# Biased maxima in two halves of the heads, the output gate beside them, and the last mixture chunks beside the first keys' products

## The chip, the core and the metric

One core of one Trainium2 chip runs the kernel. The metric is the device time in microseconds (us) of one execution. The engines have one queue each and run side by side: TensorE (PE), VectorE (DVE), ScalarE (ACT), GpSimd (POOL), and SyncE (SP), which issues the transfers. They wait for each other by semaphores only.

## The reference

Eight sequences of 512 tokens and 256 channels go through block attention, a layer norm, a mixture of experts, and a second layer norm.

```python
x = _layernorm(x + _L0_attn_ref(x, ...), axis=-1)
x = _layernorm(x + _L0_ffn_ref(x, ...), axis=-1)
# attention: 32 heads of 8 channels, chunks of 32 tokens
gate = jnp.einsum('bshd,bnhd->bhsn', q, kmean)     # own chunk always, future never
_, topk_idx = jax.lax.top_k(gate, 4)               # four chunks for each query and head
scores = jnp.where(allowed, jnp.einsum('bshd,bthd->bhst', q, k) * scale, NEG)
o = jnp.einsum('bhst,bthd->bshd', jax.nn.softmax(scores), v)
g = (hidden_states @ Wg1.T @ Wg2.T)
o = o * rms * o_norm_weight * jax.nn.sigmoid(g);  o = o @ Wo.T
# mixture: 2 shared and 16 routed experts of width 176, every expert on every token
hj = jax.nn.relu(flat @ w1 + b1); acc + (hj @ w2 + b2) * gating
```

## The kernel before

The program runs eight turns, one for each sequence. Turn b does the attention of sequence b and, woven into the same queues, the mixture of sequence m = b - 1. The first turn has no mixture (m is None), and after the eighth turn the last mixture runs alone. So seven turns have both. The order is written out by hand on each engine, and semaphores tie the queues together.

The mixture's hidden layer is cut into 25 chunks of 128 units. One chunk goes: `up`, in three parts of two products each, into one of two PSUM banks (`BK_H`, by the chunk's parity); `relu` on ScalarE; `gated` on VectorE, the multiplication with the expert's gate, whose rows come by transfer; `high` on ScalarE, the fp16 upper part; `low` on GpSimd, the rest; `down`, in four parts of three products, into the two output banks 6 and 7 (`BK_Y`).

The attention part of a turn has these stages.

- Selection of chunks (`best`, `select`), beside chunks 3 to 10.
- **Maxima**, beside chunks 11 to 21 (`C_MAX`). 40 units `max_unit` (eight groups of four heads, five units each) write query-by-key products into two pairs of banks in turn (`RING` is 2). VectorE reduces each unit to one maximum for every 32 keys (line 1356). `DEALT` lists the mixture's pieces, and `dealt(u)` is what follows unit u. `selection_rows` turns the selection's rows for the transfer.
- **The passage.** VectorE adds the selection's bias to the chunk maxima and takes the maximum, for four tiles j of 128 queries and 32 heads at once (lines 1365 and 1368). TensorE turns the four results (line 691) into PSUM, `maxima` on ScalarE copies them to `negT`, and SP moves them into the row `R_MAX` of `qET`, where the queries stand. The selection's rows go to `qET` too, once all maxima products are done (`bias_rows`). Beside it: the second factor of the output gate (line 682), its tanh (`output_gate`, line 956) and chunks 22 to 24 (`late_up`, `late_down`).
- **Keys.** 40 units `key_unit` write key-by-query products, with bias and maximum in them as extra rows. ScalarE takes the exponential (line 992, signal `act_p`), GpSimd clears what is above the diagonal (`causal`, line 1111, signal `pool_p`), and TensorE multiplies with the values (`outputs`, line 718). Two groups later `to_tokens` (line 728) turns a group's result, after VectorE has copied it (`copy_outputs`, line 1374, signal `dve_o`). `PAIRS` says which of three bank pairs a key unit uses, the third being the mixture's output banks 6 and 7; `BACK` says how many units earlier an exponential must be done. The third pair is used from group 1 on, after VectorE has read the mixture's result (`dve_z`).
- `finish` on VectorE: two reads of the mixture's result (line 1231), the layer norm's sums and inverse root, then `copy_outputs(0)`, then the scaling.

On GpSimd all `low` of a turn stand ahead of the first `stage` (line 1103, the values of a group) and `causal`.

## Time and profile before

| | us |
|---|---|
| median of 3 runs | 1453.25 (1452.52 to 1456.14) |
| the profiled execution, its own time | 1453.75 |
| its span, first to last instruction | 1451.7 |
| TensorE busy | 1332.4 (92%) |
| VectorE busy | 1087.7 (75%) |
| ScalarE busy | 842.7 (58%) |
| GpSimd busy | 533.9 (37%) |
| mean granted TensorE clock | 0.961 |

The time lies 2.05 us above the span. Busy shares are means over unlike stages; an engine of 75% can be the bound of one stage. A timeline row of several instructions gives the time from the first start to the last end. Ends of products are modelled and overlap the next start by about 0.06 us, so the cost of a piece is read from the start of one row to the start of the next. The first turn starts its keys at 122.4 us; the seven turns with a mixture follow each other at about 169 us. The last mixture alone ends at the span's end.

### The profile page before, as it was taken

How to read it: one execution, taken by the hardware profiler on the slowest of the kernel's cores; microseconds unless marked ns; L12 is line 12 of the kernel's file. 1: busy time of each engine (PE TensorE's matmuls, PEld its weight loads, DVE VectorE, ACT ScalarE, POOL GpSimd, SP SyncE). 2: the span in 40 equal slices, each digit the busy share in tenths (PEclk: the TensorE clock that was granted, in tenths of full speed). 3: DMA queues.
4: the chain of work that ended last, by engine and by line, in shares of the span. 5: the costliest groups of instructions: out<-in, count | busy, mean ns of one | idle time of the engine just before them, and what ended most of it. 6: DMA issues, size and time to landing. Idle time of an engine off the chain costs nothing.

```text
span 1451.7 us, 29057 instructions
## 1 busy us (share of the span) xinstructions
PE 1332.4 (92%) x10992; PEld 738.7 (51%) x10992; DVE 1087.7 (75%) x2747; ACT 842.7 (58%) x1266; POOL 533.9 (37%) x638
## 2 busy tenths in 40 slices
PE   5677999999998999999999999989999899999597
PEld 3422475535754366534755356543665347553364
DVE  6994688957897578966889578975889668885434
ACT  5406774396735876277743967358762877439121
POOL 3203542254323642245422553235432454225143
PEclk8667999999999999999999999999999999999799
DMA  6001022200321021210222003210112102220031
GB/s 243 16 15 17 16 79 76 52 17 16 104 66 38 30 59 60 74 31 16 82 71 55 16 17 102 71 33 30 60 62 71 31 16 68 73 53 23 13 113 58
DMA packets 52283, 77.81 MB, mean 54 GB/s; under 512 B 6334, under 2 KB 26800, under 8 KB 51888
## 3 DMA queue, kind: packets, MB, share of 16 engines
q1 hardware_dynamic: 52144, 75.96, 18.0%
q8 instruction: 87, 1.43, 0.4%
q14 instruction: 52, 0.43, 0.1%
HBM read 67.02 MB, written 8.65 MB: 52 GB/s over the span
## 4 chain that ended last, share of the span: by engine, by line
PE 61%; DVE 19%; ACT 11%; DVEq 3%; issue 3%; DMA 2%; POOL 1%; SPq 0%; POOLq 0%
PE PS L562 14%; PE PS L574 13%; PE PS L718 8%; ACT UQ L992 7%; PE PS L492 7%; PE PS L509 3%; DVE hr L1163 3%; ACT UK L992 2%; DVE CM L1356 2%; DVEq L1155 2%; PE PS L773 2%; PE PS L413 2%; DVE CM L1275 2%; PE PS L728 2%; PE PS L483 2%
## 5 line engine op out<-in xcount | busy, mean ns | idle before, releaser
L1051 POOL TENSOR_TENSOR hp<-hr,hp 128x512 f16<-128x512 f32 (+1 forms) x200 | 237.1, 1186 | 584.1 <-ACT hp L849 520.0
L1356 DVE TENSOR_REDUCE CM<-PS 128x32 f32<-128x1024 f32 x320 | 376.2, 1218 | 23.2 <-PE PS L492 18.9
L574 PE MATMUL PS<-W,hp 128*128 128x256 f16 (+1 forms) x2400 | 323.2, 274 | 4.6 <-POOL hp L1051 3.6
L562 PE MATMUL PS<-x1T,W 128*128 128x512 f16 (+1 forms) x1200 | 320.6, 385 | 0.0
L840 ACT ACTIVATE hr<-PS,CF 128x512 f32<-128x512 f32 (+1 forms) x200 | 137.2, 686 | 234.3 <-PE PS L562 234.3
L574 PEld LDWEIGHTS PS<-W,hp 128*128 128x128 f16 (+1 forms) x2400 | 216.9, 98 | 96.1 <-issue 34.7
L849 ACT ACTIVATE hp<-hr 128x512 f16<-128x512 f32 (+1 forms) x178 | 112.5, 632 | 169.3 <-DVE hr L1163 156.2
L1163 DVE TENSOR_TENSOR hr<-hr,gB 128x512 f32<-128x512 f32 x176 | 126.2, 717 | 64.9 <-ACT hr L840 58.5
L992 ACT ACTIVATE UK<-PS 128x1024 f32<-128x1024 f32 x160 | 153.0, 1037 | 11.4 <-PE PS L509 11.0
L562 PEld LDWEIGHTS PS<-x1T,W 128*128 128x128 f16 (+1 forms) x1200 | 107.7, 100 | 100.7 <-issue 34.9
L992 ACT ACTIVATE UQ<-PS 128x1024 f32<-128x1024 f32 x160 | 150.9, 1041 | 3.1 <-PE PS L509 1.4
L509 PE MATMUL PS<-qET,kz 64*128 64x512 f16 (+3 forms) x1024 | 112.2, 306 | 26.7 <-ACT UK L992 12.0
L1111 POOL TENSOR_SCALAR_AFFINE_SELECT UK<-UK 128x512 f32<-128x512 f32 x128 | 78.9, 641 | 149.4 <-ACT UK L992 149.4
L492 PE MATMUL PS<-kz,qET 64*128 64x512 f16 (+3 forms) x1024 | 130.9, 315 | 0.0
L509 PEld LDWEIGHTS PS<-qET,kz 64*128 64x128 f16 x1024 | 32.1, 94 | 167.8 <-ACT UQ L992 71.1
L1374 DVE COPY ropeb<-PS 128x512 f32<-128x512 f32 x64 | 44.3, 692 | 97.6 <-PE PS L718 97.5
L1111 POOL TENSOR_SCALAR_AFFINE_SELECT UQ<-UQ 128x512 f32<-128x512 f32 x128 | 78.8, 639 | 66.9 <-ACT UQ L992 66.9
L718 PE MATMUL PS<-UK,vst 128*9 128x512 f32 (+3 forms) x1024 | 90.5, 449 | 0.0
L718 PE MATMUL PS<-UQ,vst 128*9 128x512 f32 (+3 forms) x1024 | 83.9, 434 | 0.0
L936 ACT ACTIVATE kz<-PS 128x1024 f16<-128x1024 f16 x64 | 65.2, 1018 | 6.4 <-PE PS L462 6.4
L898 ACT ACTIVATE UK<-PS,CF 128x128 f32<-128x128 f32 x112 | 56.4, 521 | 16.4 <-PE PS L413 16.4
L939 ACT ACTIVATE qET<-PS 128x1024 f16<-128x1024 f16 x64 | 65.7, 1027 | 0.0
(150 smaller groups left out, 1793.8 us busy)
## 6 DMA issues: line engine op xcount, KB each, us to landing
gB<-gates SPq DMA_DIRECT2D x64, 256.0 KB, 3.3
gB<-gates SPq DMA_DIRECT2D x32, 224.0 KB, 2.9
gB<-gates SPq DMA_DIRECT2D x32, 192.0 KB, 2.9
gB<-gates SPq DMA_DIRECT2D x32, 160.0 KB, 2.6
xT<-in_xT SPq DMA_DIRECT2D x8, 512.0 KB, 5.8
qET<-rows SPq DMA_DIRECT2D x16, 256.0 KB, 5.2
v<-in_x SPq DMA_DIRECT2D x8, 512.0 KB, 4.1
gB<-gates SPq DMA_DIRECT2D x32, 128.0 KB, 2.9
```

Of the source, the lines that this page charges most:

```text
L492: mm = pe.matmul(PS[:, r + half, o:o + w], qET[rows, a, t * P:(t + 1) * P], kz[rows, a, 0:w], start=False, stop=True, skip_group_check=Tru ...
L509: mm = pe.matmul(PS[:, r + half, o:o + w], kz[rows, a, t * P:(t + 1) * P], qET[rows, a, t * P:S], start=True, stop=True, tile_position=(64 ...
L562: mm = pe.matmul(PS[0:w, BK_H[c % 2], :], W1[:, a, k, bass.ds(f0, w)], x1T[:, e, k, :], start=(n == 0), stop=(n == 5))
L574: mm = pe.matmul(PS[:, BK_Y + j // 2, (j % 2) * D:(j % 2 + 1) * D], hp[0:w, slot, a, j * P:(j + 1) * P], W2[0:w, e, bass.ds(c, 1), :].rear ...
L718: mm = pe.matmul(PS[32 * hh:32 * hh + HD + 1, BK_PV, t * P:S], vst[:, gs % 2, t, hh, :], PT[gs % 2][:, hh, o:o + w], start=(n == 0), stop= ...
L840: nc.scalar.activation(hr[0:w, slot, :], PS[0:w, BK_H[c % 2], :], ACT.Relu, bias=bias).then_inc(act_h, 1)
L849: nc.scalar.activation(hp[0:w, slot, 0, :], hr[0:w, slot, :], ACT.Copy).then_inc(s_high, 1)
L992: nc.scalar.activation(dst, src, ACT.Exp, scale=SCALE).then_inc(act_p, 1)
L1051: nc.gpsimd.tensor_tensor(hp[0:w, slot, 1, :], hr[0:w, slot, :], hp[0:w, slot, 0, :], ALU.subtract).then_inc(pool_hp, 1)
L1111: nc.gpsimd.affine_select(block, block, [[0, HG], [1, P]], ALU.is_ge, zero, base=0, channel_multiplier=-1).then_inc(pool_p, 1)
L1163: nc.vector.tensor_tensor(hr[:, slot, :], hr[:, slot, :], gB[:, r, :], ALU.mult).then_inc(dve_h, 1)
L1356: nc.vector.tensor_reduce(dst, src, AX.X, ALU.max).then_inc(dve_cm, 1)
```

## The change

The biased maxima are taken in two halves of 16 heads (`HALF`). The first half's four tiles are worked by VectorE behind the reductions of units 20 to 23, turned by TensorE behind chunk 19 (`AT_NEG`), copied by ScalarE and sent by SP, with its selection rows, before the gates of chunk 24. The second half's are worked behind the last reduction; VectorE itself copies the turned rows (`dve_neg`). The two halves have a semaphore each (`s_rows`): unit 0 of the keys waits for the first, unit 20 for the second.

The output gate's products and tanh move beside chunks 14 and 15 (`AT_GATE`), into the free one of the two hidden banks. Chunk 22 and the first products of chunk 23 are dealt into the maxima stage (88 pieces instead of 77). What is left of chunks 22 to 24 is written out between the units of key groups 0 and 1. VectorE takes the relu of chunk 24 and the fp16 upper parts of chunks 23 and 24 (`split=True`). The third bank pair is used from group 2 on.

```diff
+PAIRS = [n % 2 if n < 2 * NU else (2, 0, 1)[(n - 2 * NU) % 3] for n in range(TU)]
+BACK = [next((k for k in range(1, n + 1) if PAIRS[n - k] == PAIRS[n]), 0) for n in range(TU)]
-C_FIRST, C_TOPK, C_MAX, C_BIAS = (0, 3), (3, 11), (11, 22), (22, 25)
+C_FIRST, C_TOPK, C_MAX, C_LATE = (0, 3), (3, 11), (11, 23), (23, 25)
-for _c in range(1, MC):
+for _c in range(1, MC + 1):
     DEALT += [(_c, 0), (_c - 2, 4), (_c, 1), (_c - 2, 5), (_c, 2), (_c - 2, 6), (_c - 1, 3)]
-DEALT += [(MC - 2, 4), (MC - 2, 5), (MC - 2, 6)]
+AT_SEL, AT_GATE, AT_NEG = (1, 2), (3, 4), 8
+HALF = H // 2
...
+            def bias_rows(b, n):
+                pairs = slice(H // 4 * n, H // 4 * (n + 1))
+                if n == 0:
+                    sp.wait_ge(s_sel, 32 * (b + 1))
+                sp.wait_ge(pe_mx, b * TU + TU // 2 * (n + 1) + 1)
...
+                sp.wait_ge((act_neg, dve_neg)[n], b + 1)
...
+                    if m < B - 1 and c == NC - 1:
+                        bias_rows(m + 1, 0)
...
+                def maxima_rows(bank, n):
+                    pe.wait_ge(dve_bias, (2 * b + n + 1) * NT)
+                    for j in range(NT):
+                        mm = pe.transpose(PS[0:HALF, bank, j * P:(j + 1) * P], negm[:, j, HALF * n:HALF * (n + 1)], ident)
+                    mm.then_inc(pe_neg, 1)
...
+                pe.wait_ge(s_rows[0], 64 * (b + 1))
+                unit(0, 0)
+                unit(0, 1)
+                late_up(NC - 1, (0, 1))
+                unit(0, 2)
+                late_up(NC - 1, (2,))
+                late_down(NC - 3, (1,))
+                unit(0, 3)
+                late_down(NC - 3, (2, 3))
+                unit(0, 4)
+                late_down(NC - 2, (0, 1))
+                unit(1, 0)
+                late_down(NC - 2, (2, 3))
+                unit(1, 1)
...
+                maxima_rows(BK_H[1], 1)
+                unit(1, 2)
+                if m is not None:
+                    pe.wait_ge(s_hid, (m + 1) * NC + 2)
+                outputs(0, 0, 0)
+                unit(1, 3)
+                late_down(NC - 1, (0, 1))
+                outputs(0, 0, 1)
+                unit(1, 4)
+                late_down(NC - 1, (2, 3))
+                outputs(0, 0, 2)
+                outputs(0, 0, 3)
...
# VectorE, in the loop over the units and behind it
+                        if TU // 2 <= u < TU // 2 + NT:
+                            maxima(u - TU // 2, 0)
+                if m is not None:
+                    gated(m, NC - 2, (NC - 2) % 2, split=True)
                 for j in range(NT):
...
+                    maxima(j, 1)
+                if m is not None:
+                    dve.wait_ge(pe_h, m * NC + NC)
+                    dve.wait_ge(pool_hp, m * NC + NC)
+                    s_last = (NC - 1) % 2
+                    nc.vector.tensor_scalar(hr[:, s_last, :], PS[:, BK_H[s_last], :], b1[:, NC - 1:NC], 0.0, ALU.add,
+                                            ALU.max).then_inc(s_hid, 1)
+                    dve.drain()
+                    gated(m, NC - 1, s_last, split=True)
+                dve.wait_ge(pe_neg, 2 * b + 2)
+                nc.vector.tensor_scalar(negT[:, 1, :], PS[0:HALF, BK_H[1], :], 1.0 / UNIT, None, ALU.mult).then_inc(dve_neg, 1)
```

**TensorE, from the passage into the keys.** Lines are the kernel's own; a row with `x` stands for equal instructions, and the brackets name the semaphores that the first waits for. Before, `W,hp` is a `down`, `qET,kz` a key unit and `UK,vst` an `outputs`:

```order
L574 MATMUL PS<-W,hp 128x256 [waits pool_hp]
L574 MATMUL PS<-W,hp 128x256 x11
L574 MATMUL PS<-W,hp 128x256 [waits pool_hp]
L574 MATMUL PS<-W,hp 128x256 x11
L509 MATMUL PS<-qET,kz 128x512 [waits act_p,act_eg,s_rows]
L509 MATMUL PS<-qET,kz 128x512
L509 MATMUL PS<-qET,kz 128x512 [waits act_p]
L509 MATMUL PS<-qET,kz 128x512
L574 MATMUL PS<-W,hp 128x256 [waits pool_hp]
L574 MATMUL PS<-W,hp 128x256 x11
L509 MATMUL PS<-qET,kz 128x384 [waits act_p]
L509 MATMUL PS<-qET,kz 128x384
```
After the change the rows of the second half (`CF,flag`, line 674) stand behind key unit 6, the first `outputs` (line 737) behind unit 7, and the `down` of chunk 24 (line 587) behind that:

```order
L674 MATMUL PS<-CF,flag 16x128 [waits dve_bias,s_hid]
L674 MATMUL PS<-CF,flag 16x128 x3
L522 MATMUL PS<-qET,kz 128x384 [waits act_p]
L522 MATMUL PS<-qET,kz 128x384
L522 MATMUL PS<-qET,kz 128x128 x2
L737 MATMUL PS<-UK,vst 9x512 [waits pool_v,dve_o,pool_p,s_hid]
L737 MATMUL PS<-UK,vst 9x512 x3
L522 MATMUL PS<-qET,kz 128x384 [waits act_p]
L522 MATMUL PS<-qET,kz 128x384
L522 MATMUL PS<-qET,kz 128x128 x2
L587 MATMUL PS<-W,hp 128x256 [waits pool_hp]
L587 MATMUL PS<-W,hp 128x256 x5
```
The `down` of chunk 24 has moved from ahead of key unit 2 to behind key unit 8 and the first `outputs`.

**TensorE, start of key group 2 after the change.** `CF,ropeb` (line 747) is `to_tokens(0)`; before, the same rows stood in the same order, but five units further from the wait for `dve_z`, which stood at unit 5:

```order
L522 MATMUL PS<-qET,kz 128x512 [waits dve_z]
L522 MATMUL PS<-qET,kz 128x512
L522 MATMUL PS<-qET,kz 128x512 [waits act_p]
L522 MATMUL PS<-qET,kz 128x512
L522 MATMUL PS<-qET,kz 128x384 [waits act_p]
L522 MATMUL PS<-qET,kz 128x384
L522 MATMUL PS<-qET,kz 128x128 x2
L747 MATMUL PS<-CF,ropeb 128x128 [waits dve_otok,dve_o]
L747 MATMUL PS<-CF,ropeb 128x128 x3
L737 MATMUL PS<-UQ,vst 9x512 [waits dve_o,pool_v,pool_p]
```
Unit 10 (line 522, `dve_z`) is now the first to use the third bank pair, and `to_tokens(0)` follows two units later.

**VectorE, behind the last reduction.** Before, tiles of 32 heads and chunks 22 to 24 alternate, then the first read of the mixture's result:

```order
L1365 SCALAR_TENSOR_TENSOR rep<-cbias,CM 128x32x4
L1368 TENSOR_REDUCE flag<-rep 128x32
L1365 SCALAR_TENSOR_TENSOR rep<-cbias,CM 128x32x8
L1368 TENSOR_REDUCE flag<-rep 128x32
L1163 TENSOR_TENSOR hr<-hr,gB 128x512 [waits act_h,s_gB3]
L1365 SCALAR_TENSOR_TENSOR rep<-cbias,CM 128x32x12
L1368 TENSOR_REDUCE flag<-rep 128x32
L1163 TENSOR_TENSOR hr<-hr,gB 128x512 [waits act_h,s_gB0]
L1365 SCALAR_TENSOR_TENSOR rep<-cbias,CM 128x32x16
L1368 TENSOR_REDUCE flag<-rep 128x32
L1163 TENSOR_TENSOR hr<-hr,gB 128x512 [waits act_h,s_gB1]
L1231 SCALAR_TENSOR_TENSOR x1n<-x1n,PS 128x512 [waits pe_y]
```
After, from the last two tiles of the second half on: the relu (line 1415), the gate (1194), the upper part (1198), the copy of the rows (1420), the read of the result (1262):

```order
L1382 SCALAR_TENSOR_TENSOR rep<-cbias,CM 128x16x12
L1385 TENSOR_REDUCE flag<-rep 128x16
L1382 SCALAR_TENSOR_TENSOR rep<-cbias,CM 128x16x16
L1385 TENSOR_REDUCE flag<-rep 128x16
L1415 TENSOR_SCALAR hr<-PS,CF 128x512 [waits pool_hp,pe_h]
L1194 TENSOR_TENSOR hr<-hr,gB 128x512 [waits s_hid,s_gB1]
L1198 CAST hp<-hr 128x512 [waits pe_y]
L1420 TENSOR_SCALAR negT<-PS 16x512 [waits pe_neg]
L1262 SCALAR_TENSOR_TENSOR x1n<-x1n,PS 128x512 [waits pe_y]
```
The relu and upper part of chunk 24 have come to VectorE, behind all tiles, and the read of the result stands behind the wait for the turned rows.

## Rows read from the trace of the kernel before

**Rows 1.** Waits of TensorE, 781 to 812 us (fifth turn): total, times, longest.
```profile
PE PS L509 <- ACT UK L992: 1.5, 3, 0.7
PE PS L691 <- DVE flag L1368: 1.2, 1, 1.2
PE PS L509 <- ACT UQ L992: 0.7, 1, 0.7
PE PS L509 <- DMA qET<-negT: 0.5, 1, 0.5
```

**Rows 2.** Stretches: busy us and instruction counts by engine; then clock, DMA share, GB/s.
```profile
760.50:787.50 27.00, 27.00 (x212) 14.49 (x209) 26.68 (x27) 7.27 (x11) 5.85 (x6) 1.00 0.18 57
630.00:640.00 10.00, 8.44 (x76) 2.64 (x76) 5.05 (x18) 8.92 (x10) 4.58 (x10) 0.83 0.00 0
```

**Rows 3.** Timeline of TensorE, maxima stage: start, us, engine, line, [idle <-releaser].
```profile
762.79 0.28 PE L480 MATMUL PS<-CG 128*128 128x128 bf16 x2
...
763.32 0.50 PE L574 MATMUL PS<-W,hp 128*128 128x256 f16 x3
763.65 0.59 PE L562 MATMUL PS<-x1T,W 128*128 128x512 f16 x2
764.09 0.38 PE L483 MATMUL PS<-CG 128*128 128x256 bf16 x2
...
764.73 0.50 PE L574 MATMUL PS<-W,hp 128*128 128x256 f16 x3
```

**Rows 4.** Timeline of TensorE, end of the maxima and after, same turn.
```profile
786.94 0.39 PE L492 MATMUL PS<-kz,qET 64*128 64x256 f16 x4
...
791.93 1.13 PE L682 MATMUL PS<-WG,g1T 8*128 8x256 f32 x8
792.99 0.39 PE L691 MATMUL PS<-CF,flag 128*32 128x128 f32 x2
...
805.07 1.05 PE L718 MATMUL PS<-UK,vst 128*9 128x512 f32 x8
...
809.87 0.66 PE L728 MATMUL PS<-CF,ropeb 128*128 128x128 f32 x4
```

**Rows 5.** Timeline of VectorE, maxima stage, same turn.
```profile
767.98 4.61 DVE L1356 TENSOR_REDUCE CM<-PS 128x32 f32<-128x1024 f32 x4
...
787.81 1.22 DVE L1356 TENSOR_REDUCE CM<-PS 128x32 f32<-128x1024 f32 x1
```

**Rows 6.** Timeline of VectorE, end of the first turn's maxima.
```profile
111.57 2.56 DVE L1356 TENSOR_REDUCE CM<-PS 128x32 f32<-128x1024 f32 x2
114.22 0.29 DVE L1365 SCALAR_TENSOR_TENSOR rep<-cbias,CM 128x128 f32<-128x128 f16 x1
...
118.03 0.69 DVE L1368 TENSOR_REDUCE flag<-rep 128x32 f32<-128x512 f32 x1
```

**Rows 7.** Timeline of all engines, fourth turn.
```profile
619.15 1.16 POOL L1051 TENSOR_TENSOR hp<-hr,hp 128x512 f16<-128x512 f32 x1 [4.16 <-ACT hp L849]
619.63 0.82 DVE L1365 SCALAR_TENSOR_TENSOR rep<-cbias,CM 128x128 f32<-128x128 f16 x1
...
630.06 0.30 POOL L1103 TENSOR_SCALAR vst<-v 128x128 f32<-128x128 f32 x1
...
632.40 0.64 POOL L1111 TENSOR_SCALAR_AFFINE_SELECT UK<-UK 128x512 f32<-128x512 f32 x1 [2.03 <-ACT UK L992]
...
635.57 1.90 PE L718 MATMUL PS<-UK,vst 128*9 128x512 f32 x8
```

**Rows 8.** Timeline of all engines, last mixture: one chunk's scaling and split.
```profile
1424.84 0.69 DVE L1163 TENSOR_TENSOR hr<-hr,gB 128x512 f32<-128x512 f32 x1 [1.39 <-ACT hr L840]
...
1425.62 0.43 DVE L1167 CAST hp<-hr 128x512 f16<-128x512 f32 x1
1426.13 1.16 POOL L1051 TENSOR_TENSOR hp<-hr,hp 128x512 f16<-128x512 f32 x1 [1.45 <-DVE hp L1167]
```

**Rows 9.** Timeline of VectorE, mixture's end beside the keys, fifth turn.
```profile
801.51 1.28 DVE L1231 SCALAR_TENSOR_TENSOR x1n<-x1n,PS 128x512 f32<-128x512 f32 x2 [4.45 <-PE PS L574]
...
806.80 0.45 DVE L1181 SCALAR_TENSOR_TENSOR rep<-rep 128x4 f32<-128x4 f32 x1
808.37 0.69 DVE L1374 COPY ropeb<-PS 128x512 f32<-128x512 f32 x1 [1.12 <-PE PS L718]
```

**Rows 10.** Timeline of ScalarE, first keys of the first turn.
```profile
123.02 4.69 ACT L992 ACTIVATE UK<-PS 128x1024 f32<-128x1024 f32 x5 [2.60 <-PE PS L509]
```

More of the change, by code:

```diff
@@ L257, in build @@
         act_neg = sem("act_neg")
-        s_rows = sem("s_rows")
+        dve_neg = sem("dve_neg")
+        s_rows = [sem(f"s_rows{n}") for n in range(2)]
         pe_g1 = sem("pe_g1")
@@ L668, in late_up, with late_down @@
+                def late_up(c, parts):
+                    for part in parts if m is not None else ():
                         up(m, c, part)
-                def late_down(c):
-                    for j in range(NT):
+                def late_down(c, parts):
+                    for j in parts if m is not None else ():
                         down(m, c, c % 2, j)
-                if m is not None:
-                    late_up(NC - 3)
-                    late_up(NC - 2)
-                    late_down(NC - 4)
@@ L733, in group @@
                     for d in range(3):
[L734 to L736 removed]
+                        unit(g, d)
+                    to_tokens(g - 2)
                     for t in range(NT):
@@ L1096, in turn @@
                                 low(m, i * n + first + u, (first + u) % 2)
-                    for c in range(*C_BIAS):
+                    for c in range(*C_LATE):
                         low(m, c, c % 2)
```

196 lines of the change are left out of this document (89 added, 107 removed).

## The prediction

> **What bounds the kernel now.** I read the page's busy shares first: TensorE is at 92%, so idle time is worth finding only where TensorE itself waits. The waits of TensorE, limited to the passage from maxima to keys, come next. In the fifth turn TensorE waits 1.2 us there for the last tile of biased maxima, 0.5 us for the transfer of the rows, and 1.5 and 0.7 us for exponentials [rows 1]: 3.9 us in each of seven turns. The stretches then show that the stage into which work is moved is full on two engines. In 27.0 us of maxima TensorE is busy 27.0 us and VectorE 26.68 us [rows 2]. TensorE is the bound, but VectorE has nearly nothing to spare. The last view is the timeline, which gives the order in which things end at the passage.
>
> **What a mixture turn costs at the maxima.** A part of an `up` takes 764.09 - 763.65 = 0.44 us, a part of a `down` 0.33, a maxima unit 763.32 - 762.79 = 0.53 or 764.73 - 764.09 = 0.64 [rows 3]. Ahead of the last unit's end there were 33 up parts and 42 down parts; now there are 38 and 47. That is 5 x 0.44 + 5 x 0.33 = 3.85 us. The gate's products take 792.99 - 791.93 = 1.06 us [rows 4]. A half's four transposes are the four instructions that the whole took, of which a pair's row is 0.39 us long and, without the overlap, some 0.25: 0.5 us, and I allow 0.3 for changing operands. TensorE's stage grows by 5.7 us. This is moved work, all but the 0.5.
>
> VectorE gets the first half's tiles in one piece, behind units 20 to 23. The first turn has tiles of 32 heads undisturbed: 0.29 us for 128 elements, 0.69 for 512 [rows 6], so 0.155 + 0.00104 for each element. Sixteen heads give 64, 128, 192 and 256 elements: 0.22, 0.29, 0.36 and 0.42 us, each twice (bias, then maximum), 2.6 us, and with some 0.08 us behind each of eight instructions 3.3 us. The reductions' own pitch is (4.61 - 1.22)/3 = 1.13 us [rows 5]. Unit u + 2 waits for reduction u. From the start of unit 20 to that of unit 26 TensorE has six units (3.5 us), 5 up parts (2.2) and 8 down parts (2.7), 8.4 us. VectorE begins reduction 20 at 0.6 and must end reduction 24: 5 x 1.13 + 0.1 + one gate multiplication at 0.6 + 3.3 + four drains of 0.1 gives 10.7 to 11.0. TensorE stands 2.5 us. Bounds: 1.5 us if halves cost half of the whole (4.5 us of the first turn, 2.25), 3.0 if a residue on GpSimd is in the way. Behind that VectorE needs 1.31 us a unit against TensorE's 1.47, so it recovers but gives nothing back.
>
> The gate multiplication that stood ahead of the last reduction (it starts at 787.81, 0.87 us behind the start of the last products at 786.94 [rows 4, 5]) falls elsewhere, which takes 0.45 us off. The end of the last reduction, D, comes 5.7 + 2.5 - 0.45 = 7.8 us later than before.
>
> **From D to the keys.** Before, D is 787.81 + 1.22 = 789.03 and `to_tokens(0)` starts at 809.87 [rows 4, 5]: 20.8 us. From `to_tokens` on both orders are alike, and ScalarE's exponentials, at most 4.69/5 = 0.94 us each [rows 10], pace them, so I compare at this place.
>
> After, the first key units start at D. What was waited for is gone: the first half's rows were sent some ten units earlier, the second half's are wanted at unit 20 only. But the last chunk's chain is now serial on VectorE, and three things hang behind it. In us after D:
>
> - Gate and upper part of chunk 23: 0.78 from gate to cast, 0.43 cast [rows 8], to 1.3.
> - Second half's tiles, 3.3, to 4.6. GpSimd's residue of chunk 23 starts at 1.3 too. In the fourth turn a bias operation beside such a residue took 0.82 us instead of 0.29 [rows 6, 7]. I take 0.5 for that, to 5.1; without it 4.6, with a whole residue ahead 5.6.
> - Relu of chunk 24 on VectorE, 0.75, to 5.9. Gate, cast and the start of the residue, 1426.13 - 1424.84 = 1.29 [rows 8], to 7.2; residue 1.16, to 8.3.
> - GpSimd does every residue of the turn ahead of the first `stage` (0.30) and `causal` (0.64) [rows 7]: to 9.3, and TensorE starts `outputs(0, 0, 0)` at 9.4. It got there at 6.3, behind unit 7, which waits for exponential 5. **It stands 3.1 us** and ScalarE runs dry with it.
> - `outputs` 1.0, unit 8 0.3, half of the last `down` 0.7, `outputs` 0.8, unit 9 0.3, the other half 0.7: 13.2.
> - `finish` can read the result at 13.3. Unit 10 waits for the second read (1.28 long [rows 9]), about 0.7 us. But `copy_outputs(0)` stands behind the layer norm's sums: from the first read to the end of the inverse root are 806.80 + 0.45 - 801.51 = 5.74 us [rows 9]. The copy starts at 19.0 and takes 0.69. Before, it was ready at 807.25 and waited till 808.37 for TensorE. Now TensorE is past unit 12 at 15.5 and **stands some 4.3 us** for it.
>
> `to_tokens(0)` comes at 19.8, 1.0 us sooner after D than before. The turn is 7.8 - 1.0 = 6.8 us longer. A check by idle time: 2.5 + 3.1 + 0.7 + 4.3 = 10.6 us instead of 3.9, with 0.5 us of work added, is +7.2.
>
> Beside the rows stands a rule of the Trainium skill. SBUF — State Buffer, section Who interferes with whom, says that a VectorE instruction with two SBUF inputs and a GpSimd instruction that reads SBUF exclude each other, and that the one that starts first holds the port to its end. The stretched 0.82 us, ending 0.14 us behind the residue that began first, agrees [rows 7]. By the rule the second half loses 1.0 us or nothing, as the residue or the tile is first; the total would be 1498 or 1491.
>
> **The first turn** has no mixture. Its maxima are bound by VectorE already, so the first half's tiles add 3.3 us. The exponentials begin at 123.02 [rows 10] with the last reduction's end at 111.57 + 2.56 = 114.13 [rows 6], 8.9 us apart; now unit 0 needs only the last reduction but one, and they begin about 0.4 us ahead of D. Gain 9.3 - 3.3 = 6.0 us. Bounds: 3, if the half clock there makes TensorE the bound of the first two groups, and 8.
>
> What has cover: the gate's tanh and the first half's copy fall where ScalarE is busy 7.27 of 27 us [rows 2]. SP now issues two row transfers ahead of chunk 24's gates and waits there for ScalarE's copy; behind it are chunk 24's gates, not wanted for ten units. The output store and the load of x queue behind `dve_neg`, at about D + 8; both are wanted at the turn's end.
>
> **Sum.** Seven turns at +6.8 are +47.6, the first -6.0. In the fourth turn the clock was 0.83 for 10 us of the keys [rows 2] and a set of `outputs` took 1.90 us instead of 1.05 [rows 4, 7]; I take that two such turns were 1 us dearer before, -2. Together +39.6. The profiled execution took 1453.75 us, 0.5 over the median of 1453.25; on its time 1493.4, and I say 1494.
>
> **Rivals.**
>
> - *Faster: the chains end in time.* VectorE takes the first half inside its slack, and chunk 24's chain ends before TensorE needs `causal` and the copy. It decides at `to_tokens(0)`: the copy must be ready when TensorE is past unit 12. Then the 3.9 us of waits go and 0.5 us of work comes, 7 x -3.4 = -24, with the first turn -30: 1424. For it speaks only that before, the copy had 1.1 us to spare [rows 9]; against it, that the copy is tied 5.74 us behind a `down` that moves behind `outputs` of its own group. 8%.
> - *Slower, but less.* The stop at `outputs(0, 0, 0)` is short (relu at 5.9, GpSimd not in the way): everything behind moves up by 3 us, +3.8 a turn, +21 in all: 1475. Against it stands GpSimd's order. 15%.
> - *Slower, and the clock falls.* In 630 to 640 the clock was 0.83 [rows 2], behind waits like those of rows 1. Now 8 us of waits stand in some 14, ahead of work at full speed. A third of 10 us at 1.2 instead of 2.4 GHz costs 1.7 us, in each turn 12: 1506. The Trainium skill's TensorE: Matmul & The Clock Gate, section What's actually happening, says that activity releases the throttle; the row shows a fall in two turns of seven only. 17%.
> - *No change.* ScalarE's slack later in the keys takes the delay up. TensorE's own work leaves it 0.15 us a group. 5%.
>
> **Chances.** The forecast has 55%, with 1482 to 1506 as its own range. About 0.3% (4.4 us) is what a measurement of this kernel can tell from no change. Faster 8%, same 5%, slower 87%. The range that takes in the lesser and the greater loss is 1466 to 1516.
>
> **What would show it.** Right: TensorE waits for reductions of units 20 to 24, 2 to 3 us a turn; it waits 2 to 3.5 us for line 1142 (`causal`) at the first `outputs` and 3.5 to 5 us for the copy (line 1425) at the first `to_tokens`; the first turn's exponentials start at about 117 us. Wrong: the first `outputs` runs within 1 us of unit 7, or the copy waits for TensorE as before; or the maxima stage grows by less than 6 us.

## The result and the profile after: 1526.45 us, ratio 1.049

The changed kernel takes 1526.45 us (median of 4, 1523.1 to 1527.17) against 1454.7 us for the kernel before beside it (1452.52 to 1456.21): a ratio of 1.049, 95% interval 1.0467 to 1.0513. The profiled span is 1521.0 us against 1451.7, the mean granted clock 0.944 against 0.961. The direction was as predicted; the loss is 72 us where 40 were forecast, and the time lies outside the range of 1466 to 1516.

I cut each turn at four places of TensorE's timeline: the start of the first products of the maxima, of the last, of `to_tokens(0)`, and of `to_tokens(7)`. Below, "stage" is from the first to the second, "passage" to the third, "keys" to the fourth. Means over the seven mixture turns, in us:

| kernel | stage | passage | keys | sum |
|---|---|---|---|---|
| before | 52.69 | 23.35 | 31.95 | 107.99 |
| forecast (from the text ahead) | 60.9 | 21.5 | 31.95 | 114.4 |
| after | 61.55 | 23.19 | 33.51 | 118.25 |

The forecast's row comes from its last reduction 7.8 us later (8.2 at this mark), its 19.8 us from there to `to_tokens(0)`, and unchanged keys. It lies 6.4 us above the mean of before and not 6.8, because the 6.8 was read in the fifth turn, whose passage is shorter (22.93) than the mean. So a mixture turn is 10.3 us longer, not 6.4. The first turn ends 2.3 us earlier (its successor's maxima start at 224.43 instead of 226.76), not 6.0. Seven times 10.25 less 2.3 is 69.4; the spans differ by 69.3.

The waits of TensorE in the fifth turn's passage, where [rows 1] stood (total, times, longest):

```profile
PE PS L747 <- DVE ropeb L1425: 4.1, 1, 4.1
PE PS L737 <- POOL UK L1142: 3.1, 1, 3.1
PE PS L522 <- DVE x1n L1262: 0.6, 1, 0.6
```

All four old waits are gone; three new ones stand there, the very ones of the forecast (4.3, 3.1 and 0.7). Over the whole span the waits for the copy are 32.0 us (2.6 before), those for `causal` 19.4 and those for the read 4.3 us.

TensorE's timeline in that turn, answering to [rows 4], gates and maxima first:

```profile
776.73 1.13 PE L666 MATMUL PS<-WG,g1T 8*128 8x256 f32 x4
782.34 1.13 PE L666 MATMUL PS<-WG,g1T 8*128 8x256 f32 x4
796.56 0.39 PE L496 MATMUL PS<-CG 128*128 128x256 bf16 x2 [0.20 <-DVE CM L1398]
798.44 0.39 PE L499 MATMUL PS<-CG 128*128 128x256 bf16 x2 [0.30 <-DVE CM L1398]
802.60 0.29 PE L493 MATMUL PS<-CG 128*128 128x128 bf16 x2 [0.67 <-DVE CM L1398]
...
833.58 1.11 PE L737 MATMUL PS<-UK,vst 128*9 128x512 f32 x8 [3.07 <-POOL UK L1142]
...
835.16 1.46 PE L587 MATMUL PS<-W,hp 128*128 128x256 f16 x6
836.55 1.44 PE L737 MATMUL PS<-UK,vst 128*9 128x384 f32 x8
838.25 0.83 PE L587 MATMUL PS<-W,hp 128*128 128x256 f16 x6
...
845.39 1.12 PE L747 MATMUL PS<-CF,ropeb 128*128 128x128 f32 x4 [4.11 <-DVE ropeb L1425]
846.44 1.90 PE L737 MATMUL PS<-UQ,vst 128*9 128x512 f32 x8
```

The reader is to see three things. The gate's products are there twice at 1.13, in place of once. The idle time marked in the maxima is 0.20 + 0.30 + 0.67 = 1.2 us. The stall itself is longer, since a row's end is modelled: from the start of unit 20 (792.29) to that of unit 26 (802.60) are 10.3 us, and the same pieces cost 8.4 by their usual starts, so 1.9 us are lost where 2.5 were forecast. And behind each long wait the same work takes longer: six products of a `down` 1.46 us at 835.16 and 0.83 at 838.25; `outputs`' first tile 1.90 us where it takes 1.05 in [rows 4].

VectorE and GpSimd behind the last reduction (it ends at 823.44):

```profile
819.84 3.60 DVE L1398 TENSOR_REDUCE CM<-PS 128x32 f32<-128x1024 f32 x3
...
824.84 1.23 DVE L1382 SCALAR_TENSOR_TENSOR rep<-cbias,CM 128x64 f32<-128x64 f16 x1
...
828.91 0.74 DVE L1415 TENSOR_SCALAR hr<-PS,CF 128x512 f32<-128x512 f32 x1
829.82 0.69 DVE L1194 TENSOR_TENSOR hr<-hr,gB 128x512 f32<-128x512 f32 x1 [0.16 <-DVE hr L1415]
830.97 0.43 DVE L1198 CAST hp<-hr 128x512 f16<-128x512 f32 x1 [0.46 <-issue]
...
839.12 1.28 DVE L1262 SCALAR_TENSOR_TENSOR x1n<-x1n,PS 128x512 f32<-128x512 f32 x2 [7.14 <-PE PS L587]
...
844.65 0.69 DVE L1425 COPY ropeb<-PS 128x512 f32<-128x512 f32 x1
```
```profile
824.82 1.16 POOL L1082 TENSOR_TENSOR hp<-hr,hp 128x512 f16<-128x512 f32 x1 [3.01 <-DVE hp L1198]
831.47 1.15 POOL L1082 TENSOR_TENSOR hp<-hr,hp 128x512 f16<-128x512 f32 x1 [5.49 <-DVE hp L1198]
832.59 0.30 POOL L1134 TENSOR_SCALAR vst<-v 128x128 f32<-128x128 f32 x1
832.84 1.22 POOL L1142 TENSOR_SCALAR_AFFINE_SELECT UK<-UK 128x512 f32<-128x512 f32 x2
```

This is the forecast's chain: split, second half, relu, gate, split, residue, `stage`, `causal`; then read, layer norm, copy. In us behind the last reduction, forecast and measured: relu 5.1 and 5.5, residue 7.2 and 8.0, first `outputs` 9.4 and 10.1, read 13.3 and 15.7, copy 19.0 and 21.2, `to_tokens(0)` 19.8 and 21.95.

Last the stretches: ten us from `to_tokens(0)` in the fifth and the eighth turn of after, then the fifth of before (columns as in [rows 2]; the clock is the third number from the end).

```profile
845.39:855.39 10.00, 9.93 (x76) 2.76 (x76) 3.83 (x11) 5.15 (x6) 2.76 (x5) 0.69 0.15 53
...
1384.00:1394.00 10.00, 9.94 (x98) 3.11 (x100) 4.31 (x14) 6.34 (x7) 3.17 (x6) 0.83 0.16 55
```
```profile
809.87:819.87 10.00, 9.79 (x112) 3.41 (x108) 5.64 (x17) 9.92 (x12) 6.07 (x12) 1.00 0.16 54
```

TensorE is busy in both kernels, but it issues 112 products before and 76 to 100 after. The clock of this stretch is 0.69 to 0.85 in all seven mixture turns after, and 1.00 in all seven before. Busy is not fast: the clock stood at 1.2 GHz for a third to two thirds of the stretch, after 7.8 us of waits in some 15.

The seven turns of the changed kernel run the same stretch of program and differ in this clock, so they show what it costs (before, the keys take 31.9 to 32.0 us in each of the seven). By turn, the granted clock in the ten us from `to_tokens(0)`, and the length of the keys and of the passage in us:

| turn | 2 | 3 | 4 | 5 | 6 | 7 | 8 |
|---|---|---|---|---|---|---|---|
| clock | 0.85 | 0.73 | 0.75 | 0.69 | 0.85 | 0.74 | 0.83 |
| keys | 32.87 | 33.92 | 33.72 | 34.26 | 32.84 | 33.90 | 33.03 |
| passage | 23.24 | 23.31 | 21.86 | 23.61 | 23.47 | 23.58 | 23.25 |

The lower the clock, the longer the keys, without an exception. Carried on to a clock of 1.00 at the same slope the keys would take some 31.5 us (an estimate), no more than the 31.95 of before: nothing is left of their loss for another cause. The passage of the fourth turn is the odd one. There the clock stayed at 1.00 behind the wait for `causal` (655.37 to 660.87), and in the other six turns it was 0.69 over the same 5.5 us:

```profile
655.37 1.04 PE L737 MATMUL PS<-UK,vst 128*9 128x512 f32 x8 [2.85 <-POOL UK L1142]
...
656.67 0.83 PE L587 MATMUL PS<-W,hp 128*128 128x256 f16 x6
657.43 0.83 PE L737 MATMUL PS<-UK,vst 128*9 128x384 f32 x8
```
The two pieces that took 1.46 and 1.44 us in the fifth turn take 0.83 each here, behind a wait of nearly the same length, and the passage is 1.4 to 1.75 us shorter.

### The profile page after: what moved, and what is told of

Its sections match the earlier page's. It is cut to its first block, busy times and chain, and to the rows that moved or that the text cites. A ratio compares the mean times of both kernels' runs of the same rounds, so it can differ in the third digit from the quotient of the medians.

```text
span 1521.0 us, 29326 instructions
## 1 busy us (share of the span) xinstructions
PE 1375.0 (90%) x11024; PEld 743.5 (49%) x11024; DVE 1109.5 (73%) x2840; ACT 831.3 (55%) x1237; POOL 532.1 (35%) x638
## 4 chain that ended last, share of the span: by engine, by line
PE 64%; DVE 19%; DVEq 6%; issue 5%; ACT 2%; POOL 2%; DMA 0%; SPq 0%; POOLq 0%
PE PS L587 13%; PE PS L575 13%; PE PS L737 11%; PE PS L505 6%; PE PS L522 5%; PE PS L747 3%; DVEq L1381 3%; DVE CM L1398 2%; PE PS L813 2%; DVE hr L1194 2%; PE PS L426 2%; DVEq L1186 2%; PE PS L496 2%; POOL hp L1082 2%; DVE CM L1306 2%
## 5 line engine op out<-in xcount | busy, mean ns | idle before, releaser
L1398 DVE TENSOR_REDUCE CM<-PS 128x32 f32<-128x1024 f32 x320 | 383.5, 1219 | 54.2 <-PE PS L505 50.4
L587 PE MATMUL PS<-W,hp 128*128 128x256 f16 (+1 forms) x2400 | 337.5, 276 | 4.8 <-POOL hp L1082 3.5
L575 PE MATMUL PS<-x1T,W 128*128 128x512 f16 (+1 forms) x1200 | 328.6, 386 | 1.1 <-ACT flag L996 1.1
L880 ACT ACTIVATE hr<-PS,CF 128x512 f32<-128x512 f32 x193 | 132.4, 686 | 216.6 <-PE PS L575 216.6
L889 ACT ACTIVATE hp<-hr 128x512 f16<-128x512 f32 (+1 forms) x164 | 103.7, 632 | 186.6 <-DVE hr L1194 178.0
L1194 DVE TENSOR_TENSOR hr<-hr,gB 128x512 f32<-128x512 f32 x176 | 120.7, 686 | 65.5 <-ACT hr L880 59.9
L522 PE MATMUL PS<-qET,kz 64*128 64x512 f16 (+3 forms) x1024 | 115.9, 312 | 6.6 <-DVE x1n L1262 4.3
L737 PE MATMUL PS<-UK,vst 128*9 128x512 f32 (+3 forms) x1024 | 91.8, 454 | 19.4 <-POOL UK L1142 19.4
L737 PE MATMUL PS<-UQ,vst 128*9 128x512 f32 (+3 forms) x1024 | 92.8, 471 | 0.0
L747 PE MATMUL PS<-CF,ropeb 128*128 128x128 f32 x256 | 44.9, 301 | 32.4 <-DVE ropeb L1425 32.0
```

Source lines behind the costliest of these rows:

```text
L522: mm = pe.matmul(PS[:, r + half, o:o + w], kz[rows, a, t * P:(t + 1) * P], qET[rows, a, t * P:S], start=True, stop=True, tile_position=(64 ...
L575: mm = pe.matmul(PS[0:w, BK_H[c % 2], :], W1[:, a, k, bass.ds(f0, w)], x1T[:, e, k, :], start=(n == 0), stop=(n == 5))
L587: mm = pe.matmul(PS[:, BK_Y + j // 2, (j % 2) * D:(j % 2 + 1) * D], hp[0:w, slot, a, j * P:(j + 1) * P], W2[0:w, e, bass.ds(c, 1), :].rear ...
L737: mm = pe.matmul(PS[32 * hh:32 * hh + HD + 1, BK_PV, t * P:S], vst[:, gs % 2, t, hh, :], PT[gs % 2][:, hh, o:o + w], start=(n == 0), stop= ...
L880: nc.scalar.activation(hr[0:w, slot, :], PS[0:w, BK_H[c % 2], :], ACT.Relu, bias=bias).then_inc(s_hid, 1)
L889: nc.scalar.activation(hp[0:w, slot, 0, :], hr[0:w, slot, :], ACT.Copy).then_inc(s_high, 1)
```

## The experiments

Changes are to the kernel named first. Where no interval is given it was one run.

**The gate's products.** In the changed kernel they cost 2.1 us a turn (1.06 each time), before 1.06 for all four. Four forms of the kernel before ask what decides.

e1: `for j in (0, 2, 1, 3)` becomes `(0, 1, 2, 3)`; the row group is `j // 2`.

> The kernel before, with one edit: its four output gate products stand in the order 0, 1, 2, 3 instead of 0, 2, 1, 3, so that neighbours use the same eight rows of the array, as they do in the changed kernel. Theory (products of different rows run beside each other, of the same rows after each other): the eight gate instructions take 2.1 us a turn instead of 1.06, as the changed kernel shows with 2 x 1.06, and the time grows by 2 to 8 us, because a wait of 1.2 us for the last tile of maxima stands behind them and takes part of it up. Rival (the changed kernel's 2.1 us come from the other place, between mixture products): they still take 1.06 us and the time is the same within 1 us.

1453.48 us, ratio 1.0006 (0.9996 to 1.0015), and the eight entries still take 1.06 us from start to next start, as the rival had it. They start two by two in this order too (791.84 and 791.86, then 792.16 and 792.18), as they do before, so four in a row run in pairs even where two of one row group stand first; why is not shown here. e1 therefore does not show what a lone pair costs. e5 and e6 part the pairs:

```diff
-    late_down(NC - 4)
 ...
 for j in (0, 2, 1, 3):          # e5; in e6 (0, 1, 2, 3)
+    if m is not None and j == 1:    # in e6 j == 2
+        late_down(NC - 4)
```
So the tail of a chunk stands between the first pair and the second.

> The kernel before, with the down of chunk 21 standing between the two pairs of gate products instead of ahead of all four. The pairs are 0, 2 and 1, 3: two products in different rows of the array, into two banks. Theory after the last result (what matters is that two products into different banks or rows stand next to each other; the order 0, 1, 2, 3 of four in a row still had such neighbours within reach): each pair takes about 0.53 us, 1.06 in all. Rival (a block of such products costs 1.06 us however many it holds): each pair takes about 1.06 us. The time tells nothing here, the trace does.

> The same with the pairs 0, 1 and 2, 3: two products in the same rows of the array and into the same bank, as in each half of the changed kernel. Theory (same rows, one after the other): each pair takes 1.06 us, 2.1 in all, as in the changed kernel. Rival (the changed kernel's 1.06 us a half comes from its place beside the maxima): 0.53 us each.

e14 is e6 with the two products of a pair in two banks and all four from the first row group. What it leaves out is the second group: the gate of the last two token tiles is made from the rows of the first two, so its output is not the kernel's. (The edit of the tanh that reads the banks is not shown.)

```diff
-r = ROW_G1 * (j // 2)
-mm = pe.matmul(PS[:, j // 2, (j % 2) * D:(j % 2 + 1) * D], ...
+r = 0
+mm = pe.matmul(PS[:, j % 2, (j // 2) * D:(j // 2 + 1) * D], ...
```

> The kernel before with the gate products in two pairs (0,1) and (2,3) with the tail of a chunk between them, as in e6, but the two products of a pair go to two banks, and all four take their operands from the first row group. What is left out: the gate of the last two token tiles is made from the rows of the first two. Theory: two products of the same rows of TensorE run one behind the other whatever bank they write, so a pair costs 1.06 us, as in e6. Rival: in e6 it was the shared bank; then a pair costs about 0.63 us, as the pairs of two row groups did in e5.

TensorE at both pairs, e5 first, then e6, then e14 (start, us; the next row's start gives the cost):

```profile
789.42 0.70 PE L683 MATMUL PS<-WG,g1T 8*128 8x256 f32 x4
790.05 1.48 PE L574 MATMUL PS<-W,hp 128*128 128x256 f16 x12
```
```profile
790.68 1.13 PE L683 MATMUL PS<-WG,g1T 8*128 8x256 f32 x4
791.74 1.49 PE L574 MATMUL PS<-W,hp 128*128 128x256 f16 x12
```
```profile
790.88 1.13 PE L683 MATMUL PS<-WG,g1T 8*128 8x256 f32 x4
791.94 1.49 PE L574 MATMUL PS<-W,hp 128*128 128x256 f16 x12
```

0.63, 1.06 and 1.06 us, in every mixture turn of the three traces. So it is the rows and not the bank: two products of the same row group run one behind the other, in one bank or in two; two of different groups, in two banks, run beside each other. (Two groups into one bank was not run.) The Trainium skill says the same of row groups (TensorE: Matmul & The Clock Gate, section Why this matters for your kernels: small products run concurrently if each lands in a row group of its own). The change cut the gate by row group, because each half has one bank to write, and so it pays 2.1 us in place of 1.06. The times, of one run each, are 1453.44, 1454.8 and 1454.64 us beside 1454.16, 1454.16 and 1453.34 of before: no difference that could be told.

**GpSimd's order (e2).** The changed kernel with `causal(0)` ahead of the residue of chunk 24:

```diff
-                    for c in range(*C_LATE):
+                    for c in range(C_LATE[0], NC - 1):
                         low(m, c, c % 2)
...
                         causal(i * 2 + u, u)
+                        if m is not None and i == 0 and u == 0:
+                            low(m, NC - 1, (NC - 1) % 2)
```

> The changed kernel, with GpSimd clearing group 0 (causal) ahead of the residue of chunk 24 instead of behind it. Theory (GpSimd's order makes the first outputs wait): the wait for causal, 2.8 us in each of seven turns, goes; the last down then waits up to 1 us for the residue. 2 to 2.8 us a turn less, 15 to 20 us in all: about 1508. If the clock's falls came of these waits, up to 7 us more. Rival (the chain on VectorE, tiles then relu then gate, sets the passage anyway): the wait moves to the last down or to the copy of group 0, and less than 5 us are gained: above 1521.

1509.63 us, 1.0394 (1.0377 to 1.0412): 16.8 us less. The wait for `causal` is gone; TensorE waits for the residue instead, at chunk 24's `down`, 10.5 us in all against 3.5, about 1.0 a turn. The passage falls from 23.19 to 20.32.

**VectorE's order at the copy (e3, e4).** The changed kernel with the copy ahead of the layer norm:

```diff
+                if between is not None:
+                    between()
                 dve.drain()
-                layernorm(x1n, x1n, dve_out, between)
+                layernorm(x1n, x1n, dve_out)
```

> The changed kernel, with the copy of group 0's outputs straight behind VectorE's two reads of the mixture's result, ahead of the layer norm's sums. Theory: the wait of 4.4 us at the first to_tokens goes, but the sums and the scaling, 5.9 us, now stand ahead of the first keep and the second copy, and the second to_tokens waits some 2 us. 2.5 us a turn less, and 1 us of half clock: 20 to 25 us in all, about 1504. Rival (nothing comes back, because the norm is merely moved): the second to_tokens waits the whole 4 us and the time is 1520 to 1527. Third: the norm fits into VectorE's slack entirely, 30 us or more less: below 1496.

> Both edits: causal of group 0 ahead of the last residue, and the copy of group 0 ahead of the norm. Theory (two waits in series on TensorE, each with its own cause): the gains add, 35 to 50 us, 1476 to 1490, and the stretch from the first to the last to_tokens of a turn, 33.5 us now and 31.9 before the change, comes back to within 0.5 us of 31.9, because the granted clock no longer falls. Rival (one hides the other): the sum is no more than the larger of the two, and the time stays above 1495.

e3 takes 1505.24 us, 1.0357 (1.0341 to 1.0372), 21.2 less; e4, with e2's edit too, 1489.05, 1.0246 (1.0231 to 1.0261), 37.4 less. The two gains add (16.8 + 21.2 = 38.0). Counted from the kernel before as it ran beside each, which was 1.4 us quicker beside these three, they are 15.4, 19.8 and 36.0. But e4's keys take 35.79 us, where I expected them near 31.9, and the copy is still waited for 21.2 us in all. The passage fell to 16.05, 7.1 less than after, and 2.3 of it came back in the keys. The next kernels look for it.

**First guess: the norm in one piece is too long (e7).** e4 with the norm cut in three: read, copy, sums and mean; then the inverse root ahead of the pair's second `keep` and the scaling behind it.

> The changed kernel with causal of group 0 ahead of the last residue, and the mixture's layer norm cut into three: result read, copy of group 0, sums, then keep and copy of group 1, inverse root, keep, scaling. Theory (TensorE's waits of 4.4 and then 2.7 us are only VectorE's order of work; its total fits beside the keys): the first to_tokens waits under 0.5 us and the second under 1, the stretch from first to last to_tokens comes back from 35.6 to 32.0 to 32.6 us, 1458 to 1465 us. Rival (VectorE has too much work there, any order makes a later group wait): the stretch stays above 34 us and the time above 1475.

1488.69 us, 1.0233 (1.0216 to 1.025), where 1458 to 1465 was expected: a miss, nothing gained. The wait for the copy is 21.3 us, as in e4.

**The last chunk ahead of the second half (e8).** e7 with relu, gate and split of chunk 24 ahead of the second half's tiles, and their transposes behind half of chunk 24's `down`:

```diff
                     gated(m, NC - 2, (NC - 2) % 2, split=True)
-                for j in range(NT):
-                    maxima(j, 1)
...
                     gated(m, NC - 1, s_last, split=True)
+                for j in range(NT):
+                    maxima(j, 1)
```

> As the run before, and on VectorE the relu, gate and upper part of chunk 24 ahead of the second half's tiles, whose rows are not wanted before key unit 20; TensorE turns them behind the first half of the last down. Theory (what is left of the passage is the serial chain tiles, relu, gate, upper part, residue, down): the wait for the residue, 1.0 us a turn, goes, the result is read 1 to 2 us sooner, and the stretch from the last maxima unit to the first to_tokens falls from 16.0 to 14 to 15 us. 1446 to 1456. Rival (TensorE's own work sets that stretch): under 0.5 us a turn, the time is within 4 us of the run before. With the maxima stage still 8.9 us longer than before the change, both leave this kernel within 1% of the kernel before.

1480.23 us, 1.0173 (1.0154 to 1.0193). The passage is 14.97 as expected, the total (1446 to 1456) not, since the keys are 35.21. Its timeline shows why. TensorE, then VectorE, fifth turn:

```profile
828.11 0.91 PE L522 MATMUL PS<-qET,kz 64*128 64x512 f16 x8
831.51 0.65 PE L747 MATMUL PS<-CF,ropeb 128*128 128x128 f32 x4 [2.49 <-DVE ropeb L1431]
```
```profile
826.31 1.37 DVE L1225 TENSOR_SCALAR x1n<-x1n,rep 128x256 f32<-128x256 f32 x4
827.77 0.90 DVE L1454 TENSOR_TENSOR CM<-CM 128x288 f32<-128x288 f32 x1
...
830.76 0.69 DVE L1431 COPY ropeb<-PS 128x512 f32<-128x512 f32 x1
```

TensorE waits 2.49 us at the third `to_tokens` of the turn for the copy of the third group. VectorE takes that copy in the midst of the first pair's query work, and the whole pair is late by the layer norm. In the trace of before all of the norm but its scaling lay before `to_tokens(0)` and cost the keys nothing.

The wait costs more than its length here too, though not in each turn. Ten us behind it, in the second and in the fifth turn:

```profile
313.10:323.10 10.00, 9.93 (x98) 2.95 (x100) 4.18 (x15) 6.40 (x7) 3.28 (x6) 0.83 0.00 0
831.50:841.50 10.00, 9.93 (x112) 3.45 (x116) 5.51 (x18) 7.86 (x9) 4.69 (x9) 1.00 0.01 2
```
Six turns have this wait of 2.5 us. In three of them the clock is 0.83 behind it and the keys take 35.6 to 35.8 us, in three it stays at 1.00 and the keys take 34.1; the seventh turn waits 3.7 us, has 0.83 too, and takes 36.9.

**Second guess: later (e9, e10).** e8 with sums and mean ahead of the second `keep` of the second pair, inverse root and scaling ahead of that of the third. e10 adds the first half's tiles at units 20, 23, 26, 29 (`AT_NEG` 10).

> The kernel of e8 with the layer norm of the result moved out of the first pair of groups: sums and mean with variance ahead of the second keep of the second pair, inverse root and scaling ahead of the second keep of the third pair. The work is the same, only its place on VectorE differs. Theory: the 3.6 us that the keys' stretch lost (from the first to_tokens to the eighth: 34.1 to 36.9 in e8 against 31.9 before) is the layer norm's 5.6 us of VectorE in front of the copy of the fourth group, which in e8 started at 830.76 although its products had ended about 2.5 us before; in the second and third pair VectorE has some 3 us of idle time to take it. Then the stretch falls to 32 to 32.8, the wait of to_tokens for the copy falls from 21.3 us in all to under 6, and the time is 1480 minus 7 times 2.5 to 3.5, so 1455 to 1463. Rival: the stretch is long because TensorE runs at 1.2 GHz after the waits of the passage; then it stays at 34 or more, and the time at 1475 to 1481.

> The kernel of e9 with the four tiles of the first half's maxima after units 20, 23, 26 and 29 in place of 20, 21, 22 and 23, and the transposes of that half two chunks later. Theory: the four tiles in a row make VectorE late with four reductions running, which costs TensorE 0.2, 0.3 and 0.67 us per mixture turn and some 3 us in the first turn, where the units are shorter; three units apart each tile fits in the slack of VectorE. The maxima stage falls by 1.0 to 1.2 us from 61.55, the first turn's by 1.5 to 3, and the time by 8 to 12 us against e9. Rival: VectorE is the engine that sets the pace of the whole stage, so that the work only moves; then the stage stays at 61.5 and the time within 2 us of e9.

1509.71 us, 1.0389 (1.0373 to 1.0404), and 1507.16, 1.0373 (1.0355 to 1.039): e9 is 29.5 us slower than e8, where 17 to 25 less was expected, and its keys take 39.72. This was a clear miss, and the most telling one. VectorE and TensorE of e9:

```profile
848.14 1.40 DVE L1216 BATCH_NORM_STATS2 rep<-x1n 128x6 f32<-128x256 f32 x4
849.61 0.38 DVE L1219 BATCH_NORM_AGGREGATE rep<-rep 128x2 f32<-128x6 f32 x4
850.06 0.31 DVE L1439 COPY CM<-PS 128x144 f32<-128x144 f32 x1
...
852.42 0.51 DVE L1206 TENSOR_TENSOR rep<-rep 128x32 f32<-128x32 f32 x1
...
853.70 0.69 DVE L1434 COPY ropeb<-PS 128x512 f32<-128x512 f32 x1
```
```profile
854.44 0.66 PE L747 MATMUL PS<-CF,ropeb 128*128 128x128 f32 x4 [1.48 <-DVE ropeb L1434]
...
868.71 1.12 PE L747 MATMUL PS<-CF,ropeb 128*128 128x128 f32 x4 [4.77 <-DVE ropeb L1434]
```

VectorE has idle time in a pair, but not where I had put the work. Between the second `keep` and the copy of the next even group there is a chain of some 2.5 us of short steps and only 0.6 us of idle time. What stands ahead of that `keep` beyond its 0.75 us of idle time delays the copy. 1.9 us there came out as 1.48 us of wait and, in the third pair, 3.8 us (and steps that GpSimd slowed behind them) as 4.77. Spreading the tiles did what it should in the mixture turns: stage 60.98, 0.57 less (of 1.0 to 1.2), with the marked idle time of 1.2 down to about 0.5 (e10 gains 2.5 us in all on e9, where 8 to 12 were expected); in the first turn it ends 0.7 us sooner (117.60 against 118.27).

**Third guess: each piece inside a gap (e11, e12).** The gap of 2.1 us stands ahead of the copy of an odd group.

```diff
                     keep(i * 2, 0)
+                    if m is not None and i == 1:      # e12: 0
+                        norm_sums(x1n)
+                    if m is not None and i == 2:      # e12: 1
+                        inverse_root(NT, a=mv[:, :, 1], out=mv[:, :, 1])
+                    if m is not None and i == 3:      # e12: 2
+                        norm_scale(x1n, x1n, dve_out, mv)
                     copy_outputs(i * 2 + 1)
```
(Mean and variance stand behind that copy in the pair of the sums; the tiles are e10's.)

> The kernel of e8 with the first half's tiles after units 20, 23, 26 and 29 (as in e10) and the layer norm of the result cut into pieces that stand in the gap of VectorE ahead of the copy of an odd group: sums (1.4 us) in the second pair, their mean and variance (0.8) ahead of that pair's second keep, inverse root (about 1.9) in the third pair, scaling (1.4) in the fourth. Theory: VectorE had 2.1 us of idle time ahead of the odd copy, 0.75 ahead of the second keep and 0.63 ahead of the even copy in the trace of before; what e9 put ahead of the second keep (1.8 us and 5 us) was longer than the gap there and came out as 1.5 us in the second pair and 4.8 us in the third, while e7 and e8 paid 2.5 us in the first. With each piece inside a gap of 2.1 us the stretch from the first to the eighth to_tokens falls to 32 to 33, the maxima stage is 61.0 as in e10, and the time is 1480 minus 7 times 3.0 to 3.6 and 4 to 6 of the tiles: 1449 to 1456. Rival: the short steps of VectorE take 0.5 in place of 0.19 us where GpSimd's affine selects run, so the pieces overflow the gaps: stretch 34 to 36, time 1465 to 1478.

> The kernel of e11 with every piece of the layer norm one pair of groups earlier: sums ahead of the copy of the second group and mean with variance behind it, inverse root ahead of the copy of the fourth group, scaling ahead of the copy of the sixth. Theory: in e11 the stretch from the first to the eighth to_tokens was 32.7 against 31.9, with one wait of 1.3 us at the last of its to_tokens (843.23), because no key units run beside the last pair and the gap there is shorter than the scaling's 1.4 us; the first pair's gap of 2.8 us (e9's trace) was empty. Then the stretch is 31.9 to 32.1, the wait gone, and the time 5 us under e11, 1451 to 1455, within 0.3% of the kernel before. Rival: the pieces slow the first pair, since the result is only read there, and the stretch stays at 32.5 or more, the time at 1457 to 1460.

e11 takes 1457.98 us, 1.0033 (1.0023 to 1.0043), e12 1451.98, **0.9988 (0.9979 to 0.9997)**, each over 9 to 11 runs. Keys: 32.61 and 31.65 us. What was left in e11 is its last pair's scaling, which lies beside GpSimd's preparation of the next turn there and takes 0.9 us longer than in e12, where it does not; the wait it leaves at the last `to_tokens` of a turn is 1.3 us. VectorE's scaling in e11, then in e12 with the sums in their gap:

```profile
840.32 2.26 DVE L1234 TENSOR_SCALAR x1n<-x1n,rep 128x256 f32<-128x256 f32 x4
842.50 0.67 DVE L1440 COPY ropeb<-PS 128x512 f32<-128x512 f32 x1
```
```profile
808.20 1.40 DVE L1223 BATCH_NORM_STATS2 rep<-x1n 128x6 f32<-128x256 f32 x4
...
811.09 0.69 DVE L1440 COPY ropeb<-PS 128x512 f32<-128x512 f32 x1 [1.50 <-PE PS L738]
...
827.73 1.38 DVE L1234 TENSOR_SCALAR x1n<-x1n,rep 128x256 f32<-128x256 f32 x4
```

In e12 the copy waits for TensorE again ([1.50 <-PE]), not TensorE for the copy (2.9 us in all, 2.6 before). The clock beside it, ten us from the first `to_tokens`:

```profile
807.20:817.20 10.00, 9.96 (x114) 3.38 (x116) 6.23 (x22) 10.00 (x12) 5.27 (x10) 1.00 0.00 1
```

| kernel | stage | passage | keys | time |
|---|---|---|---|---|
| after | 61.55 | 23.19 | 33.51 | 1526.45 |
| e2 | 61.55 | 20.32 | 33.64 | 1509.63 |
| e3 | 61.56 | 18.45 | 35.23 | 1505.24 |
| e4 | 61.55 | 16.05 | 35.79 | 1489.05 |
| e8 | 61.55 | 14.97 | 35.21 | 1480.23 |
| e12 | 60.98 | 14.97 | 31.65 | 1451.98 |
| before | 52.69 | 23.35 | 31.95 | 1453.34 |

e12 has all that the change moves, and its time is that of before to 0.1%. The stage's 8.3 us more are the passage's 8.4 us less, most of it moved work. That the change gains nothing even so can be added up, as an estimate: the four waits of [rows 1] (3.9 us) are gone, and in their place stand 1.06 us of dearer gate, some 1.3 of stall in the maxima (1.9 less the 0.57 of the tiles), 0.6 of wait for the read and the forecast's 0.5 for four more transposes, 3.5 in all. The whole 72 us of the loss came from the order of short work on VectorE and GpSimd: the waits that it made, and the clock behind them.

## Why the prediction missed: the waits held, the clock and some sizes did not

- **The three waits: right.** At the first `outputs` 3.1 us forecast, 3.07 measured (19.4 in seven turns); for the copy 4.3 and 4.1; for the second read 0.7 and 0.6. e2 and e3 show the first two by taking away what makes TensorE wait.
- **The stage: +8.2 forecast on the marks above, +8.86 measured.** The stall was over-priced, 2.5 against 1.9 by starts; VectorE's chain was 9.6 us from the start of reduction 20 (792.93) to the end of reduction 24 (802.54), where 10.1 were forecast. The gate was under-priced: 1.06 taken from [rows 4] as one block, where the row says x8 and the change makes two of x4 from one row group each, 2.1 (e6, e14). The extra parts and transposes together are what is left, 4.8 us, where 4.65 was allowed.
- **The passage: 1.85 sooner forecast, 0.16 measured. This step failed.** Its waits were right, its work was priced at full clock: from the first `outputs` to the read 3.9 us forecast, 839.12 - 833.58 = 5.54 measured. Two sets of the rows shown there cost 0.63 (1.46 - 0.83) and, against the 0.83 that this tile takes in the fourth turn, 0.61 (1.44 - 0.83) more. The fourth turn, whose clock did not fall there, bears this out: 4.0 us from the first `outputs` to the read, and a passage of 21.86 where 21.5 was forecast. The other 0.8 us of the fifth turn is the last residue, later because gate and cast stand 1.15 us apart (0.78 in the fourth) and the tile beside the residue took the whole 1.0 us more, not 0.5.
- **The keys: no change forecast, +1.56 measured. This step failed too**, and for the same reason: the clock was 0.69 to 0.85 in every turn, and the keys' length follows it turn by turn (the table above). In the fifth turn `to_tokens` took 0.46 us more (1.12 against 0.66) and the first tile of `outputs` 0.85 more; the stretch is 34.26 there.
- **The rival of the falling clock was the right one**, at 17% and with 1.7 us a turn. The fall came in the keys of every turn, at a mean cost of 1.6 us, and in the passage of six turns, at 1.4 to 1.75. Together that is some 20 of the 72 us, by the tables above. I had the row that shows it [rows 2] and the waits that would bring it, and then used that row with the other sign, as 2 us to be given back. With that sign turned and those sizes, 1494 becomes some 1516.
- **The Trainium skill's rule on the clock** (TensorE: Matmul & The Clock Gate, section What's actually happening: activity releases the throttle) goes with this trace: the fall comes behind the waits of 3.1 and 4.1 us, and in e12, without them, the same stretch stands at 1.00. Not every turn is hit: behind waits of 2.5 us in e8 the clock fell in three turns of six, and behind those of 2.7 to 3.1 us here in six of seven. **Its rule on the port** (SBUF — State Buffer, section Who interferes with whom) agrees as well: a tile's bias at 824.84, 0.02 us behind the residue's start, took 1.23 us where it takes 0.23 beside none (794.85, first half); of the two figures I gave by that rule, 1498 was the one.
- **The first turn: -6.0 forecast, -2.3 measured.** Its stage grew by 5.6 us at its end (117.81 against 112.25), not by 3.3. The second pair of gate products took 2.0 us there at the lower clock. What the first half's tiles cost there beyond their own length was not worked out. The bound of 3 was given with that half clock as its reason and should have been taken.

Summed: 7 x (0.65 + 1.69 + 1.56) = 27.3 us of mixture turns and 3.7 of the first are 31 us more than the 1493.4 forecast for the profiled execution, so 1524.4; it took 1523.1. ScalarE also has less to do in the slow stretch (5.15 us of 10 against 9.92), but the table by turn shows that this follows from the clock. What is not settled is why the clock falls behind one wait and not behind the next of the same length, and how the first turn's 3.7 us divide.

## What to carry to other kernels

Before moving short work into a period that is paced by another engine, find in the trace the idle time that stands directly at the place where the work is to go, and keep each piece shorter than it; a sum of idle time says nothing, as e9 (+29.5 us) and e12 (-28.3 us against e8, of which the tiles are some 2.5 by e10) show. A wait on TensorE costs its own length and then, often, the work behind it at half the clock: behind 4.1 us in all seven turns, behind 2.7 to 3.1 in six of seven, behind 2.5 in three of six (e8). So such a new wait should be priced with both, here at 1.4 to 1.75 us more for each fall. When waits are right in a forecast and the total is not, cut the turn at fixed marks in both traces and compare the pieces, before looking at any further wait.
